# A graph layer on one core: six destination columns per dense tile in place of seven, 45 steps in place of 48

## The reference, cut to what matters

```
h = relu(layernorm(x))
deg = max(number of edges into each node, 1)
w = (deg[src] * deg[dst]) ** -0.5
message = (h[src] + relu(edge_attr @ W1e + b1e) @ W2e + b2e) * w        # one per edge
agg = segment_sum(message, dst)
out = relu(((1 + eps) * h + agg) @ W1n + b1n) @ W2n + b2n + h
result = x + out * rsqrt(mean(out * out) + 1.19e-7) * rms_w
```

## Time and profile before

| | |
|---|---|
| median of 3 runs | 1139.05 us |
| span of the profiled execution | 1134.4 us |
| before the edge loop | to about 99 us |
| edge loop | 99 to 1083 us |
| epilogue | the last 51 us |

### The profile page before, as it was taken

One profiled execution on the slowest core, in us unless ns is written; L12 is line 12 of the kernel. 1 busy time (PEld: TensorE's weight loads), 2 busy tenths in 40 slices (PEclk: granted clock), 3 DMA queues, 4 the chain that ended last, 5 costly groups with the idle time before them and its releaser, 6 DMA issues. The chain is left out here.

```text
span 1134.4 us, 36152 instructions
## 1 busy us (share of the span) xinstructions
PE 1029.8 (91%) x12915; PEld 815.7 (72%) x12915; DVE 934.7 (82%) x4071; ACT 730.2 (64%) x1747; POOL 792.7 (70%) x790
## 2 busy tenths in 40 slices
PE   0424999999999999999999999999999999999986
PEld 0423778788787887777778878788787887878843
DVE  6898888888888888888788888888888888888658
ACT  8953666666666666666566666666666666666435
POOL 1045777777777777777777777777777777777364
PEclk9999999999999999999999999999999999999988
DMA  6045545444554444544544445444454444543473
GB/s 226 15 178 155 153 132 156 131 128 140 135 154 134 130 140 129 156 134 129 140 135 133 137 131 156 132 130 138 130 154 132 131 140 130 156 133 72 144 268 114
DMA packets 60623, 158.50 MB, mean 140 GB/s; under 512 B 16819, under 2 KB 24550, under 8 KB 60064
## 3 DMA queue, kind: packets, MB, share of 16 engines
q1 hardware_dynamic: 35504, 103.53, 27.5%
q0 software_dynamic: 23936, 49.45, 19.7%
q10 hardware_dynamic: 1008, 3.21, 0.8%
HBM read 149.43 MB, written 6.69 MB: 138 GB/s over the span
## 5 line engine op out<-in xcount | busy, mean ns | idle before, releaser
L1051 POOL DMA_INDIRECT arena<-node_rows,idx x748 | 749.6, 1002 | 240.5 <-issue 155.7
L1222 ACT ACTIVATE arena<-bank 128x343 f16<-128x343 f32 x864 | 407.9, 541 | 281.8 <-PE bank L1127 280.4
L1277 DVE TENSOR_SCALAR arena<-iota_c,code 128x343 f16<-128x343 f16 x864 | 304.5, 426 | 0.0
L1137 PE MATMUL bank<-t_words,arena 128*126 128x256 f16 x2352 | 302.1, 275 | 0.4 <-DVE arena L1340 0.4
L1290 DVE SCALAR_TENSOR_TENSOR arena<-iota_h,hi_f,bank 128x49 f32<-128x49 f32 x864 | 178.7, 261 | 112.3 <-PE bank L1092 109.9
L1212 ACT ACTIVATE arena<-bank 128x512 f32<-128x512 f32 (+1 forms) x432 | 227.4, 573 | 65.1 <-PE bank L1077 62.4
L1137 PEld LDWEIGHTS bank<-t_words,arena 128*126 128x126 f16 x2352 | 250.6, 136 | 1.1 <-issue 0.8
L1127 PE MATMUL bank<-arena 128*128 128x343 f16 x864 | 233.4, 343 | 13.4 <-ACT arena L1222 4.2
L1077 PE MATMUL bank<-w1e,arena 64*128 64x128 f32 x3264 | 221.9, 272 | 0.0
L1077 PEld LDWEIGHTS bank<-w1e,arena 64*128 64x128 f32 x3264 | 217.8, 190 | 3.8
L1127 PEld LDWEIGHTS bank<-arena 128*128 128x128 f16 x864 | 90.6, 131 | 73.9 <-issue 38.5
(11 more groups left out here) (201 smaller groups left out, 878.1 us busy)
## 6 DMA issues: line engine op xcount, KB each, us to landing
arena<-low_src SPq DMA_DIRECT2D x50, 588.0 KB, 7.6
arena<-in_attr SPq DMA_DIRECT2D x48, 512.0 KB
arena<-in_attr SPq DMA_DIRECT2D x48, 448.0 KB
arena<-node_rows,idx POOLq DMA_INDIRECT x748
arena<-in_attr SPq DMA_DIRECT2D x48, 128.0 KB
node_rows<-arena SPq DMA_DIRECT2D x1, 3160.5 KB, 8.9
arena<-in_x ACTq DMA_DIRECT2D x7, 448.0 KB, 11.1
arena<-in_x SPq DMA_DIRECT2D x6, 512.0 KB, 12.7
```

The source lines that it names most:

```text
L1051: nc.gpsimd.indirect_dma_start(out=edge_rows[:, u, j, 0:ROW], out_offset=None, in_=table, in_offset=bass.IndirectOffsetOnAxis(ap=idx[:, c, ...
L1137: mm = nc.tensor.matmul(x_sum[0:XC, 0:2 * D], strip[:, u, k, :], T16[:, k, :], start=k == 0, stop=k == NBLK - 1)
L1222: nc.scalar.activation(strip[:, u, :, tile * W:tile * W + W], pair_bank[:, j * 512:j * 512 + CW].rearrange("p (k w) -> p k w", w=W), ACT.C ...
L1277: ins = nc.vector.tensor_scalar(code_oh[:, p % PB, j, :, 0:W], iota_c[:, :].rearrange("p (k w) -> p k w", w=W), code[:, column(c), 2 * p + ...
```

## The change

W goes from 7 to 6, and TD from 18 to 20 (120 columns per step in place of 126), TG stays 16. There are S = 45 steps of 36 tiles, and only the last 8 steps are one tile short. That gives 712 gathers. The fifth unit of dense tiles has 4 tiles in place of 2, so phase 2 takes 8 tiles in place of 6; there are ten count pairs a step in place of nine, the tenth in phase 4, and `spread_rows` is cut into 10, 2, 15, 15 and 7 matmuls in place of 8, 2, 14, 14 and 11. The windows are 96 nodes wide in place of 128. `low_oh` is made for ten tiles at a time, twice a step, in place of six tiles three times. Edge lists with tiles of up to 12 destinations now take two passes in place of all, by an added test (`bank[5]`, `drop`); lists that pass the first test take one pass as before.

```diff
-WIN = 128
+WIN = 96
-TD, TG = 18, 16
+TD, TG = 20, 16
-LOOKS = [0, 2, 4, 6, 8, 9]
-UNITS_D = [(0, 4), (4, 4), (8, 4), (12, 4), (16, 2)]
+LOOKS = [0, 2, 4, 6, 8, 10]
+UNITS_D = [(0, 4), (4, 4), (8, 4), (12, 4), (16, 4)]
-SPREAD_AT = [0, 8, 10, 24, 38, 49]
+SPREAD_AT = [0, 10, 12, 27, 42, 49]
-GROUP_AT = [0, 5, 10, 14]
+GROUP_AT = [0, 5, 10, 15]
-S = -(-TILES // (TS - 1)) - 1
+S = -(-TILES // TS)
-ATTR_PAIRS = [0, 8, 15, 17]
+ATTR_PAIRS = [0, 8, 16, 18]
-W = 7
+W = 6
-WS = W + 1
+WS = 8
-LB = 6
+LB = 10
+CHECKS = 6
...
-            for j, (limit, op) in enumerate(((W / 2, ALU.is_gt), (0.0, ALU.is_lt), (0.0, ALU.is_lt),
-                                             (float(WIN - GW + 1), ALU.is_ge), (float(GW - W), ALU.is_gt))):
-                ins = nc.vector.tensor_scalar(outside[:, j:j + 1], extreme[:, j:j + 1], limit, None, op)
-            ins.then_inc(found, 1)
+            for j, (limit, op) in enumerate(((2 * W - 0.5 - MID, ALU.is_gt), (0.0, ALU.is_lt), (0.0, ALU.is_lt),
+                                             (float(WIN - GW), ALU.is_gt), (float(GW - 2 * W), ALU.is_gt),
+                                             (float(WIN - W), ALU.is_gt))):
+                nc.vector.tensor_scalar(outside[:, j:j + 1], extreme[:, j:j + 1], limit, None, op)
+            nc.vector.tensor_scalar(outside[:, CHECKS:CHECKS + 1], extreme[:, 0:1], W / 2, None, ALU.is_gt).then_inc(found, 1)
...
-            step(nc.vector.tensor_scalar(npass_f[:, :], fast[:, :], float(1 - NPASS), float(NPASS), ALU.mult, ALU.add))
+            step(nc.vector.tensor_scalar(npass_f[:, :], bank[5][:, 0:1], 0.0, float(NPASS - 2), ALU.is_equal, ALU.add))
+            step(nc.vector.tensor_tensor(npass_f[:, :], npass_f[:, :], fast[:, :], ALU.mult))
+            step(nc.vector.tensor_scalar(npass_f[:, :], npass_f[:, :], -1.0, float(NPASS), ALU.mult, ALU.add))
+            nc.vector.tensor_scalar(drop[:, :], fast[:, :], MASKED, -float(W), ALU.mult, ALU.add)
...
                         if c > 0:
+                            after = (c - 1) * NA + j // 2 * NA // (TG // 2)
                             if j % 2:
-                                pool.wait_ge(tile_ps, 2 * ((c - 1) * NA + (j // 2 + 6)))
+                                pool.wait_ge(tile_ps, 2 * (after + 6))
...
                     if live(c) and last:
                         for k in range(UD):
                             sum_dense(c, k)
-                    if live(c) and not last:
+                    if live(c):
                         count_pair(c, u, 2 * p + 1)
...
                         if p < NPH - 1:
                             relu(c, u, 2 * p + 1)
-                            keep_counts(c, u, 2 * p + 1)
+                        keep_counts(c, u, 2 * p + 1)
...
-                nc.vector.tensor_scalar(place[:, 0, :], iota[:, :], off[:, 0, column(c)].unsqueeze(1) if isinstance(c, int)
+                nc.vector.tensor_scalar(place[:, 0, :], iota[:, 0:WIN], off[:, 0, column(c)].unsqueeze(1) if isinstance(c, int)
```

More of the change, by code:

```diff
@@ L49 @@
 FIRST_TILE = [c * TS - max(0, c - (S - SHORT)) for c in range(S + 1)]
-SLOTS_D = [(g, i) for i in range(4) for g in range(4)] + [(0, 4), (1, 4)]
+SLOTS_D = [(g, i) for i in range(5) for g in range(4)]
 SLOTS_G = [(g, i) for i in range(4) for g in range(4)]
@@ L356, in begin_gpsimd @@
             nc.gpsimd.memset(ones[:, :], 1.0).then_inc(consts, 1)
-            numbers(iota[:, :], [[1, WIN]])
+            numbers(iota[:, :], [[1, 128]])
             pool.wait_ge(consts, 3)
@@ L385, in begin_tensor @@
             pe.wait_ge(found, 1)
-            for j in range(5):
-                mm = nc.tensor.matmul(bank[4][:, 0:1], ones_bf[:, :], outside[:, j:j + 1], start=j == 0, stop=j == 4)
-            mm.then_inc(total_ready, 1)
+            for j in range(CHECKS):
+                nc.tensor.matmul(bank[4][:, 0:1], ones_bf[:, :], outside[:, j:j + 1], start=j == 0, stop=j == CHECKS - 1)
+            nc.tensor.matmul(bank[5][:, 0:1], ones_bf[:, :], outside[:, CHECKS:CHECKS + 1], start=True, stop=True).then_inc(total_ready, 1)
             pe.wait_ge(w_in, 16 * 9)
@@ L656, in build @@
         with nc.Fori(0, n_pass) as _:
[L657 removed]
+            edge_pass(nc, t, loop, table, s_kp, low_src, T16, acc, rel_s, rel_d, lo_h, iota_l, hi_f, code, s_parts, off, drop, base_f, base_i,
                       x_scale, w1e, w2e, bias_split, ones_bf, iota, iota_r, iota_c, iota_h, part_f, bank, bank2)
@@ L1273, in pair @@
                         here = here.rearrange("p o t -> p (o t)")
-                    nc.vector.tensor_tensor(low_oh[:, (u + 2 * p // LB) % 2, :, :], here.unsqueeze(1).broadcast_to((128, 128, LB)),
+                    nc.vector.tensor_tensor(low_oh[:, low_set(c, p), :, :], here.unsqueeze(1).broadcast_to((128, 128, LB)),
                                             iota_l[:, :, :], ALU.is_equal)
                 for j in range(2):
-                    ins = nc.vector.tensor_scalar(code_oh[:, p % PB, j, :, 0:W], iota_c[:, :].rearrange("p (k w) -> p k w", w=W), code[:, column(c), 2 * p + j:2 * p + j + 1],
+                    ins = nc.vector.tensor_scalar(code_oh[:, (c * NA + p) % PB, j, :, 0:W], iota_c[:, :].rearrange("p (k w) -> p k w", w=W), code[:, column(c), 2 * p + j:2 * p + j + 1],
                                                   None, ALU.is_equal)
```

32 lines of the change are left out of this document (17 added, 15 removed).

## The result

| | before | after |
|---|---|---|
| median, range (4 runs each) | 1139.4 (1137.52 to 1140.91) | 1077.92 (1073.71 to 1081.74) |
| ratio after / before | | 0.946, interval 0.944 to 0.949 |
| profiled execution: span, time | 1134.4 | 1076.9, 1078.76 |

The change makes the kernel 61.5 us faster. The direction was right, the size was not.

The account below looks back on a forecast made before the run. PE was taken as the bound, POOL's gathers as a near-bound. Step terms summed to +0.46, 20.65 us; with 43 steps for 46, the 5.8 us gone and other terms, -46.7 gave 1092.3 us; range 1080 to 1105.

Parts of the forecast that it names:

- MLP and the stall at pair 5: PE's edge MLP in phase 2 grows from 6 to 8 tiles, +0.27 us; pair 5 waits for DVE's code one-hots, +0.10.
- dense sums, two tiles more: PE's sums of dense tiles, 20 in place of 18 at 0.068 us a tile: +0.14 us a step.
- look: PE's look in phase 2, x8 in place of x4, 0.20 us against 0.11: +0.09 us a step.
- count pairs: a tenth, nine narrower, pair 4's wait: PE's count pairs: a tenth +0.34 us, nine narrower by column price -0.38, pair 4's shorter wait for ScalarE's copies -0.05.
- turn and windows: Twelve f32 instructions on PE with 96 columns: weight loads bind, so only -0.05 us a step; ends 0 and -0.33.
- spread: PE's 49 spread matmuls of 256 moving columns stay; fewer output rows change neither columns nor count: 0.
- gathered sums: PE's sums of gathered tiles in a step: no change, 0.
- one pass: The edge lists pass the tests, so the loop runs once; rival of two passes or a step beyond 21.7 us: chance 0.03.
- `low_oh` at 0.74: DVE's low one-hots for ten tiles, 1280 columns, take 0.72 to 0.77 us, against 0.46 for 768 columns.
- No wait for gathers is left: POOL lags PE 0.14 us a step, 5 us over 37 steps, within a reserve of at least 8.9; 5.8 us of waits go.
- POOL takes over: Rival: cheap windows make PE's step 20.37 us or less, 5 us of waits on gathers come back, time 1084.4; chance 0.20.
- Slow gathers: Rival: the longer `low_oh` catches POOL's gathers, 16 take 21.3 us, 12 us are lost, time 1104; chance 0.13.

Follow-up runs that it names:

- Experiments 2 and 3: 2: kernel before with W = 6 alone, 1135.2 us. 3: kernel before, code one-hots in a row, 1133.0; changed kernel with `WS = 6`, 1077.3.
- experiment 6: Changed kernel without semaphore waits ahead of gathers, ratio 0.943; short steps moved into the loop, 0.948; low one-hots for four tiles, 0.937; also combinations.
- LB = 4: Changed kernel with low one-hots made for four tiles at a time in place of ten: 1071.8 us, ratio 0.937.
- experiment 4: Changed kernel with the last two dense tiles' sums left out, 36 a step in place of 40: 1083.7 us (one run).

## Why the prediction was wrong, step by step

The terms of a step, in us, from the starts on PE where no gather is waited for:

| term | forecast | measured |
|---|---|---|
| MLP and the stall at pair 5 | +0.27, +0.10 | +0.52 |
| dense sums, two tiles more | +0.14 | +0.01 |
| look | +0.09 | +0.09 |
| count pairs: a tenth, nine narrower, pair 4's wait | +0.34 - 0.38 - 0.05 | -0.45 |
| turn and windows | -0.05 | -0.05 |
| spread | 0 | -0.07 |
| gathered sums | 0 | 0 |
| step | 20.65 | 20.24 |

- **The count pairs are the step that failed.** I priced a narrower pair by columns, 0.44 ns each, 0.042 a pair. Experiments 2 and 3 show 0.08: runs of 7 cost as 8, so two in eight go and not one in seven. That is 0.36 us a step, 15 us of the loop. The row that I used (spread, 256 even columns) could not show it, while the earlier trace rows held a warning: a pair of 343 took 0.38, 0.19 a matmul, more than the 0.15 that 0.44 ns gives. Only 0.02 of that gap is the run of 7 (0.34 in a row). The step with W = 6 alone shows the whole size: -0.83 for nine pairs. The tenth pair adds 0.31, and five pairs with low one-hots of ten tiles add 0.016 each, a term that I had at nothing (experiment 6, `LB = 4`).
- **The dense sums** were divided by tiles, where they go by units of four: 0.13 a step, 5.6 us (experiment 4).
- **The MLP** cost 0.15 more than forecast. Pair 5 stalls as said and for the reason said (0.18 idle, released by the code one-hots), and its stall sits in the slot of the MLP ahead of it; of +0.52, 0.27 are the two tiles, 0.25 the stall. `LB = 4` takes it away.
- **The look, one pass, `low_oh` at 0.74:** right. The turn and the windows too: loads bind and 0.05 is saved, though by the first matmul of either group and not the last.
- **"No wait for gathers is left"** failed, and not only because PE's step was shorter, as the text had warned ("If PE's step is shorter than I think, this cover is gone"). A mean of 20.8 for 16 gathers gives a lag of 0.56 a step, and the reserve of 10.7 would have lasted some 16 steps. In the trace the time from a step's last gather to its use falls from 10.7 at step 1 to 3.2 at step 8, 1.07 a step (in the kernel before from 8.9 to 3.4, 0.79, where the text had 0.60). Nothing is left of it at step 11, where it is 1.7, about what a gather needs to land, and 9.4 us of waits come back. An estimate from the same numbers: at the forecast step of 20.65 the gathers would have lagged 0.66 a step and used up the cover in some 14 steps, so the term would have failed with the right step too. So the rival "POOL takes over" came true, but through another cause than cheap windows, and its time of 1084 still held the dear count pairs.
- **Slow gathers:** over the whole loop the mean is that of the kernel before, 1.300 against 1.303. In the first eight steps, though, 16 gathers took 20.24 + 1.07 = 21.3 us, which is the rival's figure; later they took 20.7. `LB = 4` takes 20 ns off a gather (1.280). That long one-hots catch the gathers is not shown (experiment 6), and the slow gather of the earlier trace rows ends at 618.19, 0.8 us behind the scalings that I had put it down to.
- **Around the loop:** up to the turn of step 0 -1.8 where the text had -0.6 (+0.9 and -1.5), behind the loop -1.0 where it had +0.4; both about 1.3 us to the good side. Single profiles do not resolve this: turn 0 lies at 133.6 and 134.0 in the changed kernel's two, and at 136.0 in experiment 4, whose prologue is the same. I took the 4.65 us between the span of one execution and the median of others for an offset. In all thirteen kernels profiled since then the execution's own time is 1.7 to 1.9 above its span, so the rest was scatter between runs: 2.8 less.

From 1092.3 to the profiled 1078.8: shorter step 43 x -0.41 = -17.6, gathers +9.4, ahead of and behind the loop -2.6, offset -2.8: -13.6 of -13.5.

## What to carry to other kernels

Price a matmul by a row of its own layout, of the moving operand and of the weights, and not by a per-column price from another shape: if a row is dearer than the price you use, ask why before you use it. An engine that is busy 70% but issues without a gap is a second bound, and every microsecond that PE gains a step is worth only what it leaves; count the reserve step by step in the trace and not from a mean, for the step that the change gives and for a shorter one. Look at what the last transfer of a loop meets: in the profiles here the clock was halved for 6.8 us where PE stood still 0.6 to 0.8 us there, and for 13.7 to 20.5 us where it stood still 4.3 to 7.9.

## What the runs showed of the hardware that was not expected

- f16 moving operands in runs of 7 out of 8: 0.165 to 0.170 us from start to start for 343 columns, where 392 at 2.4 GHz are 0.163; the same 343 in a row 0.145 to 0.150; 49 runs of 6, with or without gaps, 0.125 to 0.130.
- VectorE's one-hots of 343 columns in runs of 7: 426 ns; 343 in a row 322; 294 in runs of 6 359, in a row 300. Both engines pay for short runs, by different amounts.
- f16 weights of a count pair whose elements lie 4, 6 or 10 apart: loads of 122, 130 and 144 ns, and with W = 6 pairs of 0.284, 0.291 and 0.307 us.
- f32 matmuls of 32 columns of the array, four to a unit: 36 (the last unit of two) in 1.218, 40 in 1.232 us.
- A gather issued from GpSimd costs 0.94 + 0.30 us; the 0.30 stays when its semaphore waits are taken out.
- The granted clock fell to 0.50 inside the loop too, once. In the W = 7 kernel with the one-hots in a row, PE waits 0.67 and then 1.02 us, and the pair after the one that waited takes 0.81 in place of 0.46. Eight other waits of 0.99 to 1.02 us in the same run were followed by no fall:

```profile
406.09 0.50 PE L1128 MATMUL bank<-arena 128*128 128x343 f16 x2 [1.02 <-DVE arena L1278]
...
407.15 0.81 PE L1128 MATMUL bank<-arena 128*128 128x343 f16 x2
...
412.24 0.46 PE L1128 MATMUL bank<-arena 128*128 128x343 f16 x2
```

```profile
407.00:410.50 3.50, 3.39 (x27) 2.39 (x27) 3.36 (x19) 2.32 (x8) 2.89 (x3) 0.56 0.24 59
```
